# Routing with one scan ahead of the matmuls, one mask, both choices at once, and the tile one-hots stored token tile innermost

## What is computed

```
x = hidden_states
x = x + 0.5 * ffn(layernorm(x))          # phase 0 of the code
x = x + attention(layernorm(x))
x = x + 0.5 * ffn(layernorm(x))          # phase 1 of the code

def ffn(x):                              # E, TOP_K, D, H = 8, 2, 512, 352
    scores = x @ gate_w.T + gate_b + bias
    top_scores, top_idx = top_k(scores, 2)
    gates = softmax(top_scores)
    comb = sum(one_hot(top_idx, 8) * gates[..., None], axis=1)
    h = silu(einsum('td,ehd->teh', x, w1) + b1)
    y = einsum('teh,edh->ted', h, w2) + b2
    return einsum('ted,te->td', y, comb)
```

## Time and profile before

| | us |
|---|---|
| median of 3 runs | 840.39 |
| the profiled execution | 840.2 |
| its span (first to last instruction) | 838.5 |
| busy: PE / DVE / ACT / POOL | 766.4 / 608.8 / 360.9 / 231.4 |
| granted TensorE clock over the span | 0.961 of full |
| `route` on VectorE in phase 0, L1424 to the end of L1512 | 33.71 to 60.82 |
| `route` on VectorE in phase 1, L1424 to the end of L1512 | 611.99 to 639.29 |

### The profile page before, as it was taken

How to read it: one execution, slowest core, us unless ns; L and a number is a source line. 1 busy time by engine, 2 the same in 40 slices (tenths; PEclk the granted TensorE clock), 3 DMA queues, 4 the chain that set the end, 5 groups by cost and what they waited for, 6 DMA issues and landing times.

```text
span 838.5 us, 14108 instructions
## 1 busy us (share of the span) xinstructions
PE 766.4 (91%) x4218; PEld 423.2 (50%) x4219; DVE 608.8 (73%) x1024; ACT 360.9 (43%) x626; POOL 231.4 (28%) x225
## 2 busy tenths in 40 slices
PE   8689899999997997998999999999925999999998
PEld 5345465656563444444444444445503566666663
DVE  6884756666656669999989998896876555555557
ACT  5855333444433437446534654443251333333331
POOL 3212644444532001101210211102102444444431
PEclk9899999999998998899999999999966999999999
DMA  9973648985743701610451110266463573333698
GB/s 315 402 285 136 223 149 314 335 297 163 241 160 106 182 1 51 106 46 1 83 94 26 53 24 14 63 229 148 173 253 115 183 268 120 113 116 121 223 313 305
DMA packets 44955, 137.27 MB, mean 164 GB/s; under 512 B 5488, under 2 KB 5488, under 8 KB 41584
## 3 DMA queue, kind: packets, MB, share of 16 engines
q1 hardware_dynamic: 27536, 86.38, 28.6%
q0 software_dynamic: 17376, 50.34, 21.7%
HBM read 85.32 MB, written 51.38 MB: 163 GB/s over the span
## 4 chain that ended last, share of the span: by engine, by line
PE 74%; DVE 14%; DMA 4%; ACT 3%; issue 3%; POOL 2%; SPq 0%; DVEq 0%; ACTq 0%; POOLq 0%
PE bank L653 61%; PE bank L647 5%; PE bank L746 3%; DMA space<-xn_rows,slot_src 3%; PE bank L916 2%; PE bank L832 1%; DVE space L1406 1%; DVE space L1466 1%; DVE space L1685 1%; POOL space L574 1%; DVE space L1682 1%; DMA space<-x_in 1%; DVE bst L1397 1%; PE bank L850 1%; POOL rstd L606 1%
## 5 line engine op out<-in xcount | busy, mean ns | idle before, releaser
L653 PE MATMUL bank<-space 128*128 (+3 forms) x2958 | 580.2, 349 | 22.5 <-DVE space L1470 12.8
L653 PEld LDWEIGHTS bank<-space 128*128 128x128 f16 (+1 forms) x2958 | 276.3, 99 | 270.9 <-issue 25.2
L578 POOL DMA_INDIRECT y_rows<-space,slot_dst x78 | 86.4, 1108 | 157.1 <-DVE space L1538 156.5
L574 POOL DMA_INDIRECT space<-xn_rows,slot_src x78 | 81.9, 1050 | 124.2 <-PE bank L647 65.2
L1094 ACT ACTIVATE space<-bank 128x512 f16<-128x512 f32 x78 | 46.5, 597 | 146.4 <-PE bank L647 138.1
L1538 DVE TENSOR_SCALAR space<-bank,slot_gate 128x512 f32<-128x512 f32 x78 | 58.5, 751 | 60.1 <-PE bank L653 59.2
L1525 DVE SCALAR_TENSOR_TENSOR space<-bank,space 128x352 f32<-128x352 f32 x78 | 40.9, 524 | 60.7 <-PE bank L653 46.8
L1104 ACT ACTIVATE space<-bank 128x384 f16<-128x384 f32 x78 | 38.3, 490 | 94.6 <-PE bank L746 94.6
L647 PE MATMUL bank<-ident,space 128*128 128x128 f32 x440 | 66.3, 281 | 13.3 <-DMA space<-xn_rows,slot_src 11.4
L1519 DVE TENSOR_TENSOR space<-bank,space 128x512 f16<-128x512 f32 x78 | 53.9, 691 | 33.4 <-ACT space L1094 31.0
L1682 DVE SCALAR_TENSOR_TENSOR space<-space,cang 128x512 f32<-128x512 f32 x84 | 63.0, 751 | 5.4 <-ACT space L1186 3.2
(11 more groups left out here) (199 smaller groups left out, 749.5 us busy)
## 6 DMA issues: line engine op xcount, KB each, us to landing
space<-ffn_w SPq DMA_DIRECT2D x8, 1472.0 KB, 11.2
w_saved<-space SPq DMA_DIRECT2D x8, 1472.0 KB
space<-w_saved SPq DMA_DIRECT2D x8, 1472.0 KB, 8.9
xn_rows<-space SPq DMA_DIRECT2D x8, 1024.0 KB, 7.2
space<-y_rows SPq DMA_DIRECT2D x16, 512.0 KB, 6.6
space<-x_in SPq DMA_DIRECT2D x7, 1024.0 KB, 6.8
space<-att_w SPq DMA_DIRECT2D x12, 518.0 KB
space<-y_rows POOLq DMA_DIRECT2D x6, 1024.0 KB, 9.2
```

The source lines that it names most:

```text
L574: gp.indirect_dma_start(dst, None, rows, bass.IndirectOffsetOnAxis(ap=index, axis=0)).then_inc(done, 16)
L578: gp.indirect_dma_start(y_rows, bass.IndirectOffsetOnAxis(ap=slot_dst[:, t:t + 1], axis=0), yo[:, t % 2], None).then_inc(y_st[t % 2], 16)
L653: last = pe.matmul(dst, a, b, start=(n == 0), stop=(n == len(terms) - 1))
```

## The change

- VectorE writes `M8` expert by expert (`[E, NT]`) and runs the scan over the tiles on its own partition's one-hots, ahead of TensorE's products: `SC` is now the running sum of one partition.
- TensorE multiplies `SC` with `ones` into bank 4 (the running counts over all partitions; its last column is the expert's total) and raises `s_count`. Then it puts `ones` x `SC` and `others` x `M8` into bank 3 and raises a new `s_rank`. `others` holds -1 on and below the diagonal, so the sum is the rank of each token in its expert. The copy, the scan and the subtraction behind the products, and the sum of `EX` and the parts' starts, go.
- One instruction less in the search for the second best (the mask to zero, L1433).
- Both choices' slot numbers in one product and one sum of 256 elements.
- `OHhi`, `OHtok` and `OHgate` are stored slot tile by token tile (`[39, 16]`, token tile innermost) instead of `[16, 39]`. Their instructions compare with a table `tiles16` of slot tile numbers, repeated 16 times in half precision, which GpSimd writes by an iota of 640 elements ahead of the gathers, once for each phase. TensorE's moving operand of 39 columns is then read with a step of 16 elements.
- `s_ohs` is raised after each choice, and TensorE waits for each choice's 16 products apart.
- The last two experts' running counts are copied from bank 4 to `SCL` right after the one-hots.

The core of the diff:

```diff
-            select(before[:, :], ones[:, :], ALU.is_gt, 0.0, 0, [[1, P]], -1)
+            seq(gp.memset(others[:, :], 0.0))
+            select(others[:, :], others[:, :], ALU.is_gt, -1.0, 0, [[1, P]], -1)
...
+            def tile_numbers(ph):
+                count(tiles16[ph], 0, [[1, HI_PAD], [0, NT]], 0).then_inc(s_tiles, 1)
...
             more_constants()
+            tile_numbers(0)
             slots(0)
...
+            gp.wait_ge(c_out, NT)
+            tile_numbers(1)
             slots(1)
...
-                chosen = M8.rearrange("p a b -> p (a b)")
-                products(bank[3][:, 0:NT * E], [(before[:, :], chosen)])
-                products(bank[4][:, 0:NT * E], [(ones[:, :], chosen)]).then_inc(s_count, 1)
+                chosen, summed = (x.rearrange("p a b -> p (a b)") for x in (M8, SC))
+                products(bank[4][:, 0:NT * E], [(ones[:, :], summed)]).then_inc(s_count, 1)
+                products(bank[3][:, 0:NT * E], [(ones[:, :], summed), (others[:, :], chosen)]).then_inc(s_rank, 1)
...
-                pe.wait_ge(s_ohs, ph + 1)
-                products(bank[5][:, 0:SLOT_TILES],
-                         [(OHlo[ph][:, k, t, :], OHtok[ph][:, k, t, 0:SLOT_TILES]) for k in (0, 1) for t in range(NT)]).then_inc(s_inv, 1)
+                for k in (0, 1):
+                    pe.wait_ge(s_ohs, 2 * ph + k + 1)
+                    for t in range(NT):
+                        last = pe.matmul(bank[5][:, 0:SLOT_TILES], OHlo[ph][:, k, t, :], OHtok[ph][:, k, 0:SLOT_TILES, t],
+                                         start=k + t == 0, stop=k == 1 and t == NT - 1)
+                last.then_inc(s_inv, 1)
...
-                         [(OHlo[ph][:, k, t, :], OHgate[ph][:, k, half * NT + t, 0:SLOT_TILES])
+                         [(OHlo[ph][:, k, t, :], OHgate[ph][:, k, half, 0:SLOT_TILES, t])
...
-                seq(v.scalar_tensor_tensor(S2.rearrange(flat), OH1.rearrange(flat), 0.0, S.rearrange(flat), ALU.is_equal, ALU.mult))
-                seq(v.scalar_tensor_tensor(S2.rearrange(flat), OH1.rearrange(flat), -3.0e38, S2.rearrange(flat), ALU.mult, ALU.add))
+                seq(v.scalar_tensor_tensor(S2.rearrange(flat), OH1.rearrange(flat), -3.0e38, S.rearrange(flat), ALU.mult, ALU.add))
...
-                v.tensor_tensor(M8, OH1, OH2, ALU.add).then_inc(s_onehot, 1)
+                seq(v.tensor_tensor(M8.rearrange("p e t -> p t e"), OH1, OH2, ALU.add))
+                v.tensor_tensor_scan(SC.rearrange(flat), restart[:, :, :].rearrange(flat), M8.rearrange(flat), 0.0,
+                                     ALU.mult, ALU.add).then_inc(s_onehot, 1)
...
                 v.wait_ge(s_count, ph + 1)
-                seq(v.tensor_copy(CE, bank[4][:, 0:NT * E].rearrange("p (t e) -> p e t", e=E)))
-                seq(v.tensor_tensor_scan(SC.rearrange(flat), restart[:, :, :].rearrange(flat), CE.rearrange(flat), 0.0, ALU.mult, ALU.add))
-                ch(v.tensor_tensor(EX, SC, CE, ALU.subtract))
-                seq(v.tensor_scalar(tl, SC[:, :, NT - 1], 1.0, float(P - 1), ALU.max, ALU.add))
+                counts = bank[4][:, 0:NT * E].rearrange("p (e t) -> p e t", e=E)
+                seq(v.tensor_scalar(tl, counts[:, :, NT - 1], 1.0, float(P - 1), ALU.max, ALU.add))
...
-                seq(v.tensor_tensor(EX, EX, eb(base8), ALU.add))
-                seq(v.tensor_tensor(QP, bank[3][:, 0:NT * E].rearrange("p (a b) -> p a b", b=E),
-                                    EX.rearrange("p e t -> p t e"), ALU.add))
-                for k, oh_ in ((0, OH1), (1, OH2)):
-                    seq(v.tensor_tensor(KEY, QP, oh_, ALU.mult))
-                    seq(v.reduce_sum(posf[:, k], KEY, AX))
+                v.wait_ge(s_rank, ph + 1)
+                seq(v.tensor_tensor(QP, bank[3][:, 0:NT * E].rearrange("p (e t) -> p t e", e=E),
+                                    base8.unsqueeze(1).to_broadcast([P, NT, E]), ALU.add))
+                seq(v.tensor_tensor(QOH, QP.unsqueeze(1).to_broadcast([P, 2, NT, E]), OH12, ALU.mult))
+                seq(v.reduce_sum(posf, QOH, AX))
...
+                v.wait_ge(s_tiles, ph + 1)
...
-                    seq(v.tensor_tensor(OHhi[ph][:, k, :, 0:SLOT_TILES], hi16[:, k].unsqueeze(2).to_broadcast([P, NT, SLOT_TILES]),
-                                        lane16[:, 0:SLOT_TILES].unsqueeze(1).to_broadcast([P, NT, SLOT_TILES]), ALU.is_equal))
-                    last = v.tensor_tensor(OHtok[ph][:, k, :, 0:SLOT_TILES], OHhi[ph][:, k, :, 0:SLOT_TILES],
-                                           toks[:, k].unsqueeze(2).to_broadcast([P, NT, SLOT_TILES]), ALU.mult)
+                    seq(v.tensor_tensor(OHhi[ph][:, k, 0:SLOT_TILES], hi16[:, k].unsqueeze(1).to_broadcast([P, SLOT_TILES, NT]),
+                                        tiles16[ph][:, 0:SLOT_TILES], ALU.is_equal))
+                    last = v.tensor_tensor(OHtok[ph][:, k, 0:SLOT_TILES], OHhi[ph][:, k, 0:SLOT_TILES],
+                                           toks[:, k].unsqueeze(1).to_broadcast([P, SLOT_TILES, NT]), ALU.mult)
+                    last.then_inc(s_ohs, 1)
+
+                ch(v.tensor_copy(SCL, counts[:, E - 2:E]))
...
-                        last = v.tensor_tensor(OHgate[ph][:, k, half * NT:(half + 1) * NT, 0:SLOT_TILES], OHhi[ph][:, k, :, 0:SLOT_TILES],
-                                               gpart[:, half, k].unsqueeze(2).to_broadcast([P, NT, SLOT_TILES]), ALU.mult)
+                        last = v.tensor_tensor(OHgate[ph][:, k, half, 0:SLOT_TILES], OHhi[ph][:, k, 0:SLOT_TILES],
+                                               gpart[:, half, k].unsqueeze(1).to_broadcast([P, SLOT_TILES, NT]), ALU.mult)
```

More of the change, by code:

```diff
@@ L119, in build @@
         ones = sb("ones", [P, P])
-        before = sb("before", [P, P])
+        others = sb("others", [P, P])
         headmean = sb("headmean", [P, P])
@@ L201, in build @@
             OHlo.append(at([2, NT, P], F16))
-            OHhi.append(at([2, NT, HI_PAD], F16))
-        OHtok = [lay2([2, NT, HI_PAD], F16)]
+            OHhi.append(at([2, HI_PAD, NT], F16))
+        OHtok = [lay2([2, HI_PAD, NT], F16)]
         assert lay2.at <= 0
@@ L206, in build @@
         apiece = lay([PIECE])
-        OHgate = [lay([2, 2 * NT, HI_PAD], F16)]
+        OHgate = [lay([2, 2, HI_PAD, NT], F16)]
         lay = Layout(max(late.at, moe_at + NCH * TPC * D + 2 * KD * PAIR))
-        S, S2, OH1, OH2, KEY, M8, QP = (lay([NT, E]) for _ in range(7))
-        raws_first = Layout(lay.at - 6 * NT * E)([PAIR], rows=E)
-        CE, SC, EX = (lay([E, NT]) for _ in range(3))
+        S, S2, KEY, QP = (lay([NT, E]) for _ in range(4))
+        raws_first = Layout(lay.at - 3 * NT * E)([PAIR], rows=E)
+        OH12, QOH = (lay([2, NT, E]) for _ in range(2))
+        OH1, OH2 = OH12[:, 0], OH12[:, 1]
+        M8, SC = (lay([E, NT]) for _ in range(2))
+        SCL = lay([2, NT])
         m1, m2, k1, dm, th = (lay([NT]) for _ in range(5))
@@ L317, in build @@
         s_count = sem("s_count")
+        s_rank = sem("s_rank")
+        s_tiles = sem("s_tiles")
         s_ohs = sem("s_ohs")
@@ L1464, in route @@
                 seq(v.scalar_tensor_tensor(lo16, hi_f, -float(P), posf, ALU.mult, ALU.add))
+                v.wait_ge(s_tiles, ph + 1)
                 for k in (0, 1):
-                    ch(v.tensor_tensor(OHlo[ph][:, k], lo16[:, k].unsqueeze(2).to_broadcast([P, NT, P]),
-                                       lane16[:, :].unsqueeze(1).to_broadcast([P, NT, P]), ALU.is_equal))
-                    seq(v.tensor_tensor(OHhi[ph][:, k, :, 0:SLOT_TILES], hi16[:, k].unsqueeze(2).to_broadcast([P, NT, SLOT_TILES]),
-                                        lane16[:, 0:SLOT_TILES].unsqueeze(1).to_broadcast([P, NT, SLOT_TILES]), ALU.is_equal))
-                    last = v.tensor_tensor(OHtok[ph][:, k, :, 0:SLOT_TILES], OHhi[ph][:, k, :, 0:SLOT_TILES],
-                                           toks[:, k].unsqueeze(2).to_broadcast([P, NT, SLOT_TILES]), ALU.mult)
-                    if k == 0:
-                        ch(last)
-                last.then_inc(s_ohs, 1)
+                    own = NT
+                    ch(v.tensor_tensor(OHlo[ph][:, k, 0:own], lo16[:, k, 0:own].unsqueeze(2).to_broadcast([P, own, P]),
+                                       lane16[:, :].unsqueeze(1).to_broadcast([P, own, P]), ALU.is_equal))
+                    seq(v.tensor_tensor(OHhi[ph][:, k, 0:SLOT_TILES], hi16[:, k].unsqueeze(1).to_broadcast([P, SLOT_TILES, NT]),
[4 more added lines that the diff above has]
+                ch(v.tensor_copy(SCL, counts[:, E - 2:E]))
                 seq(v.tensor_tensor(cmp, lane[:, 0:SLOT_TILES].unsqueeze(2).to_broadcast([P, SLOT_TILES, E]),
@@ L1504, in route @@
                 ch.wait()
-                seq(v.tensor_scalar(posf, SC[:, E - 2:E], 63.5, 1.0 / P, ALU.add, ALU.mult))
+                seq(v.tensor_scalar(posf, SCL, 63.5, 1.0 / P, ALU.add, ALU.mult))
                 seq(v.tensor_scalar(posf, posf, MAGIC, MAGIC, ALU.add, ALU.subtract))
```

7 lines of the change are left out of this document (3 added, 4 removed).

## The result

The change makes the kernel slower: 844.53 us as the median of nine runs (841.4 to 846.58), against 840.2 for nine runs of before on the same chip (839.42 to 841.66). The ratio is 1.0044, with a 95% interval of 1.0027 to 1.0061. The prediction said 837.1, in a range of 835.6 to 841.6; the time lies outside, at the place of rival A and beyond it. The profiled execution took 844.53 us (span 842.7), that of before 840.2 (838.5): 4.3 us are to be explained.

What follows compares the result with a forecast made beforehand. It took phase 1's routing as bound by VectorE's chain, and phase 0's as VectorE and TensorE level. Phase 1's -3.65 and phase 0's +0.4 made -3.25 us: 837.1 as a median, range 835.6 to 841.6 for 8 in 10.

Steps and rivals of the forecast that it cites:

- rival A: TensorE pays for the step: 65 ns a product, 160 products on both phases' path, +5.6 us, time 842.6; chance 0.20.
- a term that the sum put at nothing: TensorE's stepped products: no added cost in the sum, 64 gate products per phase at 30 ns each, 1.9 us.
- signs of being wrong: Phase 0 moving by more than 1 us either way, or TensorE's strided products costing over 10 ns each.
- The gain of phase 1: Phase 1's routing to first slot tile: 3.65 us gained, with `slot_src` 3.4 us earlier.
- the write of `M8` with a step: VectorE in phase 1's routing: costs between 0 and 0.08 us; taken as 0.
- the wait for `s_inv`: VectorE at L1481 in phase 1 no longer waits for TensorE: -0.29 + 0.11 for a copy = -0.18 us.
- The one-hots, forecast at 0.49: VectorE's tile one-hots of 624 elements: 0.49 us instead of 0.81; four ahead of `slot_src` save 1.28 us.
- rival C: VectorE's tile one-hots stay at 0.81 us; phase 1 gains only 2.1 us, time 838.6; chance 0.10.
- step 8: Phase 1's first slot tile: VectorE ready 4.7 us earlier, the gather's side only 3.4, so L1519 starts near 635.8.
- Phase 0's +0.4: Phase 0's routing: TensorE's later start and extra product delay the 32 products and `slot_src` by 0.4 us.
- the two values that the prediction weighed: Phase 0's delay: about 0.3 us if the clock rises at the same moment, 0.65 if it rises equally later.
- The page's rule: SBUF works in 16-byte lines, each new line pays a penalty of unstated size, and striding is free over "8 bf16".

Runs made afterwards that it cites:

- groups of two: The change with tile one-hots stored in groups of two token tiles, so TensorE's step is 4 bytes: 837.56 us, ratio 0.9971; run again 836.43, ratio 0.9973.
- the series with a step of 4: Kernel before plus nine unused series of 32 TensorE products at various steps (860.26 us, single execution); at 4 elements, 39 columns took 38 ns a product.
- groups of four: The change with tile one-hots stored in groups of four token tiles, so TensorE's step is 4 elements, 8 bytes: 838.14 us, ratio 0.9982.

## Why the prediction was wrong

**The step that failed** is a term that the sum put at nothing: TensorE's read of its moving operand with a step of 16 elements. The forecast rested on 64 gate products in 1.9 us, 30 ns each; they took 4.67 us, 73 ns each. The prediction had the mechanism as rival A and gave it 0.20; more on this below. Of the signs of being wrong that it named, products with a step at over 10 ns more each is the one that came.

**The gain of phase 1 was right.** Forecast -3.65, profile -3.33. From the routing's start to `slot_src` it took 20.81 us before and 17.60 after, 3.21 less, where 3.4 was forecast. Two small terms make the difference: the write of `M8` with a step costs 0.09 (0.38 against the 0.29 of the earlier trace rows), at the upper end of the bounds given, and the wait for `s_inv`, forecast to go, is still 0.28, since the last 16 products take 1.33 us and no longer fit under VectorE's 1.2. The one-hots, forecast at 0.49, take 0.48, so rival C is refuted, and by that the double rate that the prediction cited from the Trainium skill's "VectorE: DVE Perf Modes", section "The perf-mode tier table", is borne out. L1530 waiting for ScalarE, as step 8 had it, is in the rows. The kernel with groups of two is nearly the one that the forecast had in mind, with the one-hots at 0.48 us and next to no price on TensorE: its medians lie 2.6 and 3.5 us under those of before, where -3.25 was forecast.

**Phase 0's +0.4 is neither shown nor refuted.** The first low piece starts 6.69 us after the routing begins, before 6.04: +0.65, the upper of the two values that the prediction weighed, and every kernel with the change's program up to there has it (6.68 to 6.70; 6.04 in all three with that of before). But the moment at which the clock rises covers it. In the pair of profiles above it rises in the stretch of 45 to 46 us, before in that of 42 to 43, which makes the other 0.66 of the second line. Over all profiles it rose anywhere from 42.8 to 46.2 us, with either program, and the 32 products started 19.1, 19.9 and 20.1 us after the routing began with the program of before, and 19.0 to 20.4 with that of the change. Both of the prediction's values took the moment of the rise from one execution.

**Why rival A got only 0.20: the argument against it.** The prediction had the right mechanism there, with a price of 65 ns a product, worked out from VectorE's L1457. What spoke against A in the text was that TensorE's 30 ns were its weight loads and the columns only 16, so that "twice the time per column would fit nearly whole". Twice would have: the series with a step of 4, at 0.97 ns a column, adds 13 ns to a product, and in place the 64 of groups of four took no longer than those of before (2.48 us, before 2.49). But the time per column went from at most 0.65 ns (25 / 39) to 1.87, over four times the 0.42 of a 2.4 GHz column, and reached far past the cover. (The 0.42 is in the profile after: a product of 512 contiguous 16-bit columns at full clock starts 0.21 to 0.22 us ahead of the next instruction.) The place where I could have known better is in the prediction itself: VectorE's price for a step was 0.6 ns on each element, an engine with 1.04 ns for one; the prediction gave no reason why a memory that gives an element with a step every 1.67 ns to one engine should give it to TensorE in 0.8.

The terms of A as it came: 32 products of phase 0 on the path, +1.53 from their start to `slot_src` (3.08, before 1.55; A had 32 x 35 = 1.1); 64 gate products in each phase, +2.2 each (4.67 to the next instruction, before 2.49 and 2.46; A had 64 x 35 = 2.24). That the last two agree is luck: the products took 73 ns and not 65, and before they took 39 and not 30, pauses included. On top of A came the clock: what stands behind the 64 loses 1.2 to 2.4 us where it falls, which no rival had. In the ledger this makes +1.53 in the second line, 2.2 and 1.4 in the third, of which 0.4 is given back later, and 2.2 in the last.

**Something gave back a part.** The last line is only +0.74, though it holds 2.2 us of gate products. In before, TensorE waited 1.13 us there for a gather, ahead of the fifth slot tile (two of the expectations above call it the third):

```profile
659.07 0.66 PE L647 MATMUL bank<-ident,space 128*128 128x128 f32 x4 [1.13 <-DMA space<-xn_rows,slot_src]
```

and after the change it does not wait there: a transfer had more time to land, and hid as much of the price. This wait differs by itself: in the kernels with no step of 16 in phase 1 it was between nothing and 1.13 us. In the change run again the clock fell behind the 64, and the line read 204.31, +5.2 over before and 4.5 over the first profile. Of the 4.5, 1.7 is the clock behind the 64; 1.8 comes at the very end, behind the start of TensorE's last series (17.7 us to the end in place of 15.9), and is not the layout's, since the kernel with groups of two in phase 1 and the step of 16 in phase 0 has 17.4 there. So the first profile, which kept its clock behind the 64, shows the smaller loss, but not by all of the difference.

**The page's rule.** The Trainium skill, "SBUF — State Buffer", section "Door 1: The DMA port swizzle", has lines of 16 bytes and a penalty for each new one. The runs bear that out as a count of lines: 39 columns at a step of 4 elements are 19.5 lines, and 19.5 x 1.87 = 36 ns, measured 38; at 8 elements and above each column is a line of its own, and the price stays the same, 73 and 69; at 2 elements it is 9.75 lines, 18 ns, which fits under the 25 of the series with no step. Its words on how far one may step for free are not borne out: 8 elements cost the whole price, and 4 cost half.

## What to carry over

When a layout makes one engine's elementwise work cheaper, count what the other reader of the buffer does with it, in lines of memory touched and not in elements: TensorE paid 1.8 to 1.9 ns for each, where its columns cost 0.42. A group of two or four elements innermost gave VectorE all of its double rate, and TensorE read groups of two at full speed and groups of four at half the price; such a middle is worth looking for before choosing a side. And where a risk has the same cause as a row in the trace, price it at that row's size and let the cover be shown to hold it; "it would fit" was said of twice the time. And an event that no instruction of yours sets off, such as the rise of the clock, needs more than one profile before a term can be built on its moment.

## What was new of the hardware

- TensorE's moving operand in 16-bit with a step: 25, 25, 38, 73, 73 and 69 ns for 39 columns at steps of 2, 4, 8, 16, 32 and 64 bytes. The price is nearly the same at either clock level (73 ns with 1.00 granted at a step of 8 elements, 69 with 0.50 at a step of 32).
- The granted clock fell in or behind 7 of 8 series of 64 such products, though the trace has TensorE busy without a gap, and that costs 1.2 to 2.4 us of what follows. The cause is open.
- VectorE runs a product or comparison with two 16-bit inputs at the double rate (624 elements in 0.48 us, before 0.81) when the innermost run is 16, 4 or only 2 elements long, with one input repeated in a dimension further out.
- VectorE's write of 128 f32 with a step of 16 elements takes 0.38 us against 0.29; the read of a PSUM bank in another order than it is stored (L1468) takes 0.29, nothing more.
